# Where the expert weights' three loads stand at the end of the attention heads

## The chip, the core and the metric

The kernel runs on one core of a Trainium2 chip. TensorE (PE) multiplies and transposes, VectorE (DVE), ScalarE (ACT) and GpSimd (POOL) do the rest, and SyncE (SP) only issues DMAs. ACT and POOL issue DMAs too, between their own instructions and in order with them. The metric is the device time of one launch in microseconds, lower is better.

## The reference, cut to what matters

Two layers over x of shape (16, 256, 128), 4096 tokens. Each layer has an attention part and a feed-forward part, each added back to x under a gate. The first layer's attention has 16 heads of 8 dimensions with relative positions; its feed-forward part is a mixture of 8 experts, 2 of them chosen for each token:

```python
ctx = jnp.einsum('bhts,bshd->bthd', attn, v).reshape(b, t, d)
return ctx @ Wout.T + bout                       # first layer, attention
...
logits = xf @ router_w.T                         # router_w (8, 128)
g = jnp.einsum('nd,ehd->neh', xf, w_gate)        # w_gate (8, 256, 128) f32, 1 MiB
u = jnp.einsum('nd,ehd->neh', xf, w_up)          # w_up   (8, 256, 128) f32, 1 MiB
h = jax.nn.silu(g) * u
y = jnp.einsum('neh,edh->ned', h, w_down)        # w_down (8, 128, 256) f32, 1 MiB
```

The second layer has linear attention with four 128x128 weights and biases, and a feed-forward part with its own weights. They come much later in the kernel.

## The kernel before, in words

**Heads.** The 16 heads run one after the other on PE. Head h has 16 steps: `scores` (L1159, L1163), ACT's exponential (L858), and products with the values, `context_part` (L1181), after steps 11 and, for the head before, 3. Maxima for later heads (L1132, L1134, reduced by DVE in L1691, negated in L1700) are woven in; ACT sends the negated maxima into row 96 of the operand XC in two halves (`shift_row`, L816, tile name NEG), and the scores of steps 0 and 4 wait for them. The last maximum of the last head is the 8 H-th `max_mm`.

**Normalisation.** When the context of head h is complete, DVE copies it from PSUM to EV (`evacuate_context`, L1711). The copy waits until the numerators of head h - 2 have left the same buffer (`num_out`). Then for heads 0 to 14 POOL runs a chain, `sums_to_dram(h)` and `normalise(h)`:

1. the sums go to DRAM (L621) and come back spread over 128 partitions as RC (L623);
2. DVE takes the reciprocal (L1716). In DVE's program it stands at step 11 of head h + 1, behind that head's work, and for head 14 just ahead of `evacuate_context(15)`;
3. the reciprocals go to DRAM (L629) and come back broadcast over 32 partitions in four DMAs of 128 KB (L632);
4. POOL multiplies (L635, which counts `norm_done`) and sends the numerators to R1 in four DMAs (L638).

POOL begins the chain of head h + 1 only after that of head h.

**The tail.** Head 15 has the same chain with SP as the issuer: L496, L499, reciprocal L1784, L502, four broadcasts L506, DVE's multiplication L1787 (`t_norm`), and L510 for the numerators (`t_num_out`). After it ACT copies the context into OB (L877), PE applies the output projection (L1220), and the residual and the second layernorm follow.

**Expert weights.** After the last maximum SP issues at one go: the gate weights (L481), the up weights (L482), the down weights (L483), the router (L485), and eight small loads of the second layer (L487 to L491). All four expert loads count `ld_moe`, and PE waits for all of them once, ahead of its transposes (L1210, 12 chunks of four: 0 to 3 gate, 4 to 7 up, 8 to 11 down; then the router, L1213). For each chunk ACT makes the high part (L868, `m_ev`) and DVE the low part (L1778, `w_low`); two PSUM banks alternate, so PE's chunk c waits for the low part of chunk c - 2. DVE's order there is: `evacuate_context(15)`, low parts 0 to 3, reciprocal L1784, low parts 4 to 7, multiplication L1787, low parts 8 to 11, router. The operand buffers that WGN, WUN and WDN overlay are free from the last maximum on.

After L510 SP loads the second layer's feed-forward weights into FN (L517 to L520).

Of the kernel before, what the change touches and what calls it, by code (L numbers as in the profile page):

```python
# [22 lines left out]
H, DH = 16, 8  # L23
# [4 lines left out]
HID, E = 256, 8  # L28
# [57 lines left out]
def adaln_program(nc, a, out):  # L86
# [11 lines left out]
    def sb(name, shape, dt, ctx):  # L98
        return ctx.enter_context(nc.sbuf_tensor(name, shape, dt))

    def sem(name):
        return outer.enter_context(nc.semaphore(name))

    with outer:
# [12 lines left out]
        RN = sb("RN", [E, 128], F32, outer)  # L117
# [4 lines left out]
        WGN, WUN, WDN = (YY[:, N * i:N * i + N].bitcast(F32).rearrange("p (k d) -> p k d", k=16) for i in range(3))  # L122
# [68 lines left out]
        L1W = L1V[:, 0:512].rearrange("p (w d) -> p w d", w=4)  # L191
        BKV, BO1, BQ1 = L1V[:, 512:768], L1V[:, 768:896], L1V[:, 896:897]
# [49 lines left out]
        den_out, den_in, rec_ready, rec_out, rec_in, norm_done, num_out = (sem(s) for s in (  # L242
            "den_out", "den_in", "rec_ready", "rec_out", "rec_in", "norm_done", "num_out"))
        t_den_out, t_den_in, t_rec_out, t_rec_in, t_norm, t_num_out = (sem(s) for s in (
            "t_den_out", "t_den_in", "t_rec_out", "t_rec_in", "t_norm", "t_num_out"))
        o_in, o_mm, o_add = sem("o_in"), sem("o_mm"), sem("o_add")
        ld_moe, ld_l1, ld_ff = (sem(s) for s in ("ld_moe", "ld_l1", "ld_ff"))
        m_tr, m_ev, lg_mm, cmb = sem("m_tr"), sem("m_ev"), sem("lg_mm"), sem("cmb")
        gu_mm, sg_done, h_done, y_mm, acc_done = (sem(s) for s in ("gu_mm", "sg_done", "h_done", "y_mm", "acc_done"))
        l_q, l_ex, l_qd, l_kv, l_kvd, l_kk, l_kkd = (sem(s) for s in (  # L250
# [73 lines left out]
        def _(sp):  # L324
# [136 lines left out]
            for h in range(1, H):  # L461
# [12 lines left out]
                if h + 1 < H:  # L474
# [3 lines left out]
                    score_queries(h + 1)  # L478

            sp.wait_ge(max_mm, 8 * H)  # L480
            sp.dma_start(WGN[:, :, :], a["L0_ffn_w_gate"].rearrange("e (c p) d -> p (e c) d", p=128)).then_inc(ld_moe, 16)  # L481
            sp.dma_start(WUN[:, :, :], a["L0_ffn_w_up"].rearrange("e (c p) d -> p (e c) d", p=128)).then_inc(ld_moe, 16)  # L482
            sp.dma_start(WDN[:, :, :].rearrange("p (e c) k -> p e (c k)", e=E),  # L483
                         a["L0_ffn_w_down"].rearrange("e d k -> d e k")).then_inc(ld_moe, 16)
            sp.dma_start(RN[:, :], a["L0_ffn_router_w"]).then_inc(ld_moe, 16)  # L485
            for i, w in enumerate(("wq", "wk", "wv", "wo")):
                sp.dma_start(L1W[:, i, :], a["L1_attn_" + w]).then_inc(ld_l1, 16)  # L487
            sp.dma_start(BQ1, a["L1_attn_bq"].rearrange("(p o) -> p o", o=1)).then_inc(ld_l1, 16)
            sp.dma_start(BKV[:, 0:128], a["L1_attn_bk"].partition_broadcast(128)).then_inc(ld_l1, 16)
            sp.dma_start(BKV[:, 128:256], a["L1_attn_bv"].partition_broadcast(128)).then_inc(ld_l1, 16)  # L490
            sp.dma_start(BO1, a["L1_attn_bo"].partition_broadcast(128)).then_inc(ld_l1, 16)  # L491

            h, p = H - 1, (H - 1) % 2
            sp.wait_ge(ev_done, H)
# [14 lines left out]
            for g in range(4):  # L509
                sp.dma_start(R1[DH * h:DH * h + DH, :].rearrange("p (c g x) -> p c g x", c=4, g=4)[:, :, g],  # L510
                             EV[p][32 * g:32 * g + DH, :].rearrange("p (c x) -> p c x", c=4)).then_inc(t_num_out, 16)

            sp.wait_ge(zeroed, 9)
            for k, w in enumerate(("gate", "up")):
# [250 lines left out]
        def _(act):  # L765
# [96 lines left out]
                        shift_row(h + 1, (u - 3) // 3)  # L862

            for c in range(12):
                act.wait_ge(m_tr, c + 1)
                w, k4 = c // 4, slice(4 * (c % 4), 4 * (c % 4) + 4)
                t = banks[4 + c % 2][:, :].rearrange("p (w i) -> p w i", w=4)
                A(W2[w][:, 0, k4, :], t, ACT.Copy, scale=WS).then_inc(m_ev, 1)  # L868
# [172 lines left out]
        def _(pe):  # L1041
# [158 lines left out]
            context_part(H - 1, 1, 0)  # L1200
            context_part(H - 1, 1, 1)

            pe.wait_ge(ld_moe, 64)
            pe.wait_ge(max_done, 8 * H)
            for c in range(12):
                if c >= 2:
                    pe.wait_ge(w_low, c - 1)
                src = (WGN, WUN, WDN)[c // 4]
                for j in range(4):
                    last = tr(banks[4 + c % 2][:, 128 * j:128 * j + 128], src[:, 4 * (c % 4) + j, :], ident)  # L1210
                last.then_inc(m_tr, 1)
# [921 lines left out]
```

## Time and profile before

| what | before |
|---|---|
| median of 3 runs | 1026.28 us (1025.95 to 1028.13) |
| the profiled execution's own time | 1022.87 us |
| its span, first to last instruction | 1021.0 us |
| PE busy | 823.6 us (81%) |
| DVE busy | 722.0 us (71%) |
| ACT busy | 537.6 us (53%) |
| POOL busy | 410.8 us (40%) |
| mean granted TensorE clock | 0.912 of full speed |

Start times are microseconds from the start of the span. The heads end and the experts begin between about 420 and 505 us. The profiled execution is 3.41 us shorter than the median of the timed runs; differences within the profile are compared with each other, and carried over to the median.

### The profile page before, as it was taken

To read this page: it belongs to the slowest core of one execution; us is meant where nothing else is said; L and a number is where in the kernel's file an instruction comes from. 1 tells how busy PE (TensorE), PEld (TensorE's weight loads), DVE (VectorE), ACT (ScalarE), POOL (GpSimd) and SP (SyncE) were. 2 spreads that over 40 slices of the span, in tenths; PEclk is the share of its full clock that TensorE was granted. 3 is DMA by queue.
4 is the path that set the end of the run, shared out by engine and by line. 5 is a ranking of instruction groups with operands and counts; after the bars stand their busy time and mean duration, and the time that the engine had idled before them with its cause. 6 is when DMAs were issued, how large, how long until landed. Compare 5 with 4: busy or idle time off the path is not lost.

```text
span 1021.0 us, 23783 instructions
## 1 busy us (share of the span) xinstructions
PE 823.6 (81%) x9611; PEld 599.3 (59%) x9611; DVE 722.0 (71%) x1458; ACT 537.6 (53%) x985; POOL 410.8 (40%) x473
## 2 busy tenths in 40 slices
PE   2494699999999999975479998999998785257773
PEld 1253578888787878754246655666665474135563
DVE  6976366655555555325778898788787688899994
ACT  3860365767666766345445556566564644313332
POOL 5451724443344334344333235334443127214544
PEclk9696699999999999976599999999999798579998
DMA  8037523432343333631000000000000000000111
GB/s 137 11 76 240 131 54 77 100 84 68 78 100 82 72 73 82 164 84 32 1 1 2 2 1 1 2 1 2 1 2 2 0 1 1 0 1 11 21 22 32
DMA packets 55986, 47.17 MB, mean 46 GB/s; under 512 B 22284, under 2 KB 45012, under 8 KB 55156
## 3 DMA queue, kind: packets, MB, share of 16 engines
q1 hardware_dynamic: 36816, 26.24, 11.3%
q0 software_dynamic: 7424, 13.60, 5.6%
q10 hardware_dynamic: 11636, 5.80, 2.3%
q8 instruction: 76, 1.25, 0.5%
q14 instruction: 34, 0.28, 0.1%
HBM read 30.52 MB, written 12.06 MB: 42 GB/s over the span
## 4 chain that ended last, share of the span: by engine, by line
PE 52%; DVE 27%; DMA 5%; issue 5%; POOL 4%; ACT 4%; SPq 2%; POOLq 0%; DVEq 0%; ACTq 0%
PE PS L1159 12%; PE PS L1276 5%; PE PS L1278 5%; PE PS L1277 5%; PE PS L1163 5%; PE PS L1181 5%; PE PS L1132 5%; PE PS L1134 3%; DVE XX L1559 2%; DVE HB L1953 2%; PE PS L1076 2%; DVE XX L1565 2%; DVE AM L1550 2%; DVE ACC L1945 1%; DVE HQ L2082 1%
## 5 line engine op out<-in xcount | busy, mean ns | idle before, releaser
L1691 DVE TENSOR_REDUCE MX<-PS 128x4 f32<-128x1024 f32 x128 | 156.4, 1224 | 123.0 <-PE PS L1134 122.6
L858 ACT ACTIVATE REG<-PS 128x1024 f32<-128x1024 f32 x128 | 130.2, 1018 | 132.1 <-PE PS L1163 120.9
L1159 PE MATMUL PS<-XX,TB 96*128 96x64 f16 x2048 | 160.9, 247 | 5.8 <-issue 3.9
L683 POOL TENSOR_TENSOR HH<-HB,HH 128x512 f16<-128x512 f32 x64 | 75.5, 1180 | 172.4 <-ACT HH L909 172.4
L1159 PEld LDWEIGHTS PS<-XX,TB 96*128 96x128 f16 x2048 | 121.5, 120 | 34.8 <-issue 13.0
L939 ACT ACTIVATE SG<-PS 128x512 f32<-128x512 f32 x128 | 76.2, 595 | 110.6 <-PE PS L1278 110.3
L1953 DVE SCALAR_TENSOR_TENSOR HB<-PS,SG 128x512 f32<-128x512 f32 x128 | 87.8, 686 | 44.4 <-ACT SG L939 44.3
L1163 PE MATMUL PS<-XX,KC 97*128 97x128 f16 x1024 | 107.5, 228 | 0.0
L1276 PE MATMUL PS<-XH,XX 128*128 128x512 f16 x256 | 98.5, 385 | 10.1 <-DVE HB L1953 9.9
L1277 PE MATMUL PS<-XH,XX 128*128 128x512 f16 x256 | 97.9, 382 | 0.0
L1278 PE MATMUL PS<-XH,XX 128*128 128x512 f16 x256 | 97.8, 382 | 0.0
L1132 PE MATMUL PS<-TM,YY 64*64 64x256 f16 x1024 | 81.8, 335 | 18.3 <-DVE YY L1733 9.8
L831 ACT ACTIVATE YY<-YY,CON 128x256 f16<-128x256 f16 x224 | 96.2, 497 | 0.0
L1276 PE MATMUL PS<-XX,HH 128*128 128x128 f16 x512 | 89.7, 220 | 7.3 <-issue 2.7
L1278 PE MATMUL PS<-XX,HH 128*128 128x128 f16 x512 | 89.8, 220 | 0.0
L1277 PE MATMUL PS<-XX,HH 128*128 128x128 f16 x512 | 89.8, 220 | 0.0
L909 ACT ACTIVATE HH<-HB 128x512 f16<-128x512 f32 x128 | 79.8, 623 | 7.9 <-DVE HB L1953 7.6
L1440 PE MATMUL PS<-YY,XT 128*128 128x352 f32 x128 | 49.5, 536 | 35.7 <-DVE HQ L2082 35.7
L1163 PEld LDWEIGHTS PS<-XX,KC 97*128 97x128 f16 x1024 | 76.2, 113 | 0.0
L1132 PEld LDWEIGHTS PS<-TM,YY 64*64 64x64 f16 x1024 | 50.7, 187 | 34.1 <-issue 13.5
L1134 PE MATMUL PS<-KM,YY 64*64 64x256 f16 x1024 | 69.6, 287 | 0.0
L1945 DVE SCALAR_TENSOR_TENSOR ACC<-PS,CMBT,ACC 128x128 f32<-128x128 f32 x224 | 62.8, 344 | 1.1 <-PE PS L1278 0.9
(237 smaller groups left out, 1721.2 us busy)
## 6 DMA issues: line engine op xcount, KB each, us to landing
REG<-inverse_sums POOLq DMA_DIRECT2D x60, 128.0 KB, 2.9
KC<-keys_strips SPq DMA_DIRECT2D x16, 192.0 KB
keys_strips<-REG ACTq DMA_DIRECT2D x12, 224.0 KB
R<-in_L_attn_x SPq DMA_DIRECT2D x32, 64.0 KB, 3.6
XX<-NEG ACTq DMA_DIRECT2D x120, 1.0 KB, 2.2
R<-REG POOLq DMA_DIRECT2D x60, 32.0 KB, 2.8
queries_position<-REG ACTq DMA_DIRECT2D x2, 896.0 KB
XX<-queries_position SPq DMA_DIRECT2D x56, 32.0 KB
```

Of the source, the lines that this page charges most:

```text
L831: last = A(to, queries, ACT.Copy, scale=CON[:, C_OWN + 8 - 8 * (piece // 8) + j:C_OWN + 9 - 8 * (piece // 8) + j])
L858: A(P[jt][:, 1024 * up:1024 * up + 1024].rearrange("p (k x) -> p k x", k=2), ST[u % 2], ACT.Exp).then_inc(exp_done, 1)
L909: A(HH[k % 4][:, 0, :], HB[k % 2][:, :], ACT.Copy).then_inc(hi_done, 1)
L1132: mm(o, yp[rows, a], TM[p][rows, 31 - a:31 - a + T], start=True, stop=False)
L1134: last = mm(o, yc[rows, a], KM[p][rows, :], start=False, stop=True)
L1159: mm(o_pos[:, a], TB[p][0:96, y0:y0 + 128], xp[0:96, 8 * bank + a], start=(a == 0), stop=False, skip_group_check=True)
L1163: last = mm(o[:, 128 * c:128 * c + 128].rearrange("p (b s a) -> p b s a", b=4, s=4), KC[p][0:97, c, 128 * jt:128 * jt + 128], xc[0:97, c, ...
L1276: mm(o, w[0], x[0], start=first, stop=False)
L1277: mm(o, w[0], x[1], start=False, stop=False)
L1278: return mm(o, w[1], x[0], start=False, stop=final)
L1691: nc.vector.tensor_reduce(MX[h % 2][:, :].rearrange("p (r a) -> p r a", r=2)[:, :, 2 * g:2 * g + 2], PS[:, bank:bank + 2, :].rearrange("p ...
L1953: STT(HB[k % 2][:, :], banks[2 + k % 2], 1.0 / WS, SG[k % 2][:, :], ALU.mult, ALU.mult).then_inc(hb_done, 1)
```

## The change

`ld_moe` becomes three semaphores. SP still issues the gate weights after the last maximum, and the router right behind them. It then waits for `norm_done` of 14, that is until POOL has multiplied head 13, and issues the up weights. The down weights are issued by ACT, between its high parts of chunks 3 and 4, after a wait for `norm_done` of 15 (head 14 multiplied). The eight small loads of the second layer move behind the tail's last DMA (L510), ahead of the FN loads. PE waits for gate and router before chunk 0, for up before chunk 4, and for down before chunk 8.

```diff
@@ sync
             sp.wait_ge(max_mm, 8 * H)
-            sp.dma_start(WGN[:, :, :], a["L0_ffn_w_gate"].rearrange("e (c p) d -> p (e c) d", p=128)).then_inc(ld_moe, 16)
-            sp.dma_start(WUN[:, :, :], a["L0_ffn_w_up"].rearrange("e (c p) d -> p (e c) d", p=128)).then_inc(ld_moe, 16)
-            sp.dma_start(WDN[:, :, :].rearrange("p (e c) k -> p e (c k)", e=E),
-                         a["L0_ffn_w_down"].rearrange("e d k -> d e k")).then_inc(ld_moe, 16)
-            sp.dma_start(RN[:, :], a["L0_ffn_router_w"]).then_inc(ld_moe, 16)
-            for i, w in enumerate(("wq", "wk", "wv", "wo")):
-                sp.dma_start(L1W[:, i, :], a["L1_attn_" + w]).then_inc(ld_l1, 16)
-            sp.dma_start(BQ1, a["L1_attn_bq"].rearrange("(p o) -> p o", o=1)).then_inc(ld_l1, 16)
-            sp.dma_start(BKV[:, 0:128], a["L1_attn_bk"].partition_broadcast(128)).then_inc(ld_l1, 16)
-            sp.dma_start(BKV[:, 128:256], a["L1_attn_bv"].partition_broadcast(128)).then_inc(ld_l1, 16)
-            sp.dma_start(BO1, a["L1_attn_bo"].partition_broadcast(128)).then_inc(ld_l1, 16)
+            sp.dma_start(WGN[:, :, :], a["L0_ffn_w_gate"].rearrange("e (c p) d -> p (e c) d", p=128)).then_inc(ld_gate, 16)
+            sp.dma_start(RN[:, :], a["L0_ffn_router_w"]).then_inc(ld_gate, 16)
+            sp.wait_ge(norm_done, H - 2)
+            sp.dma_start(WUN[:, :, :], a["L0_ffn_w_up"].rearrange("e (c p) d -> p (e c) d", p=128)).then_inc(ld_up, 16)
...
                 sp.dma_start(R1[DH * h:DH * h + DH, :].rearrange("p (c g x) -> p c g x", c=4, g=4)[:, :, g],
                              EV[p][32 * g:32 * g + DH, :].rearrange("p (c x) -> p c x", c=4)).then_inc(t_num_out, 16)
+            for i, w in enumerate(("wq", "wk", "wv", "wo")):
+                sp.dma_start(L1W[:, i, :], a["L1_attn_" + w]).then_inc(ld_l1, 16)
+            sp.dma_start(BQ1, a["L1_attn_bq"].rearrange("(p o) -> p o", o=1)).then_inc(ld_l1, 16)
+            sp.dma_start(BKV[:, 0:128], a["L1_attn_bk"].partition_broadcast(128)).then_inc(ld_l1, 16)
+            sp.dma_start(BKV[:, 128:256], a["L1_attn_bv"].partition_broadcast(128)).then_inc(ld_l1, 16)
+            sp.dma_start(BO1, a["L1_attn_bo"].partition_broadcast(128)).then_inc(ld_l1, 16)
@@ scalar
             for c in range(12):
+                if c == 4:
+                    act.wait_ge(norm_done, H - 1)
+                    act.dma_start(WDN[:, :, :].rearrange("p (e c) k -> p e (c k)", e=E),
+                                  a["L0_ffn_w_down"].rearrange("e d k -> d e k")).then_inc(ld_down, 16)
                 act.wait_ge(m_tr, c + 1)
@@ tensor
-            pe.wait_ge(ld_moe, 64)
             pe.wait_ge(max_done, 8 * H)
             for c in range(12):
                 if c >= 2:
                     pe.wait_ge(w_low, c - 1)
+                if c == 0:
+                    pe.wait_ge(ld_gate, 32)
+                elif c % 4 == 0:
+                    pe.wait_ge((ld_up, ld_down)[c // 4 - 1], 16)
```

## Rows read from the trace of the kernel before

**Rows 1.** The chain that ended last, 400 to 520 us: start, us, what
```profile
422.45 5.36 DMA inverse_sums<-RC
...
429.56 8.95 DMA REG<-inverse_sums
...
449.22 1.90 DMA sums<-REG
451.14 3.55 DMA RC<-sums
454.71 0.36 DVE RC L1784
455.09 1.41 DMA inverse_sums<-RC
...
467.91 1.07 ACT REG L877
```

**Rows 2.** Timeline of POOL, 427 to 461 us: start, length, idle before and releaser
```profile
428.09 1.96 POOL L632 DMA_DIRECT2D REG<-inverse_sums  x4 [5.08 <-DMA inverse_sums<-RC]
438.58 2.36 POOL L635 TENSOR_TENSOR REG<-REG 128x1024 f32<-128x1024 f32 x1 [8.53 <-DMA REG<-inverse_sums]
441.23 2.25 POOL L638 DMA_DIRECT2D R<-REG  x4 [0.29 <-POOL REG L635]
443.47 0.58 POOL L621 DMA_DIRECT2D sums<-REG  x1
445.86 0.60 POOL L623 DMA_DIRECT2D RC<-sums  x1 [1.81 <-DMA sums<-REG]
448.41 0.56 POOL L629 DMA_DIRECT2D inverse_sums<-RC  x1 [1.95 <-DVE RC L1716]
450.40 1.96 POOL L632 DMA_DIRECT2D REG<-inverse_sums  x4 [1.42 <-DMA inverse_sums<-RC]
455.21 2.35 POOL L635 TENSOR_TENSOR REG<-REG 128x1024 f32<-128x1024 f32 x1 [2.85 <-DMA REG<-inverse_sums]
```

**Rows 3.** DMA queues, 422 to 425, then 425 to 428 us: packets, MB, share
```profile
q1 hardware_dynamic: 368, 0.75, 95.9%
...
q1 hardware_dynamic: 441, 0.87, 103.3%
q0 software_dynamic: 32, 0.02, 2.4%
```

**Rows 4.** DMA queues, 428 to 433, then 433 to 436 us
```profile
q1 hardware_dynamic: 1134, 1.38, 104.8%
q10 hardware_dynamic: 320, 0.00, 4.2%
...
q0 software_dynamic: 181, 0.51, 70.8%
q1 hardware_dynamic: 365, 0.23, 35.3%
```

**Rows 5.** Timeline of PE about the end of the heads
```profile
432.45 0.34 PE L1159 MATMUL PS<-XX,TB 96*128 96x64 f16 x3 [0.98 <-DMA XX<-NEG]
...
443.77 1.93 PE L1181 MATMUL PS<-REG,V 128*32 128x256 f32 x32 [1.11 <-ACT REG L858]
...
455.67 1.97 PE L1210 MATMUL PS<-CON,YY 128*128 128x128 f32 x8 [1.33 <-DVE XX L1778]
```

**Rows 6.** Timeline of DVE, 447 to 464 us, and where FN is first read
```profile
447.76 0.35 DVE L1716 RECIPROCAL RC<-RC 128x32 f32<-128x32 f32 x1 [14.99 <-DMA RC<-sums]
...
458.30 0.69 DVE L1778 SCALAR_TENSOR_TENSOR XX<-PS,XX 128x512 f16<-128x512 f32 x1 [0.16 <-ACT XX L868]
461.46 1.23 DVE L1787 TENSOR_TENSOR REG<-REG 128x1024 f32<-128x1024 f32 x1 [2.47 <-DMA REG<-inverse_sums]
...
561.42 0.95 DVE L1550 TENSOR_REDUCE YY<-YY 128x48 f32<-128x768 f32 x1
```

**Rows 7.** Timeline of SP's queue, 420 to 467 us
```profile
420.52 0.84 SPq L481 DMA_DIRECT2D YY<-in_L_ffn_w_gate  x1
...
424.12 3.43 SPq L483 DMA_DIRECT2D YY<-in_L_ffn_w_down  x1
...
429.38 0.43 SPq L487 DMA_DIRECT2D YY<-in_L_attn_wk  x1
...
456.52 1.71 SPq L506 DMA_DIRECT2D REG<-inverse_sums  x4
```

**Rows 8.** ACT: its timeline at chunk 4; lines L845, L952 (ns min/median/max, starts)
```profile
453.52 0.60 ACT L868 ACTIVATE XX<-PS 128x512 f16<-128x512 f32 x1 [1.08 <-PE PS L1210]
...
L845 ACTq DMA_DIRECT2D queries_position<-REG x2: 808/860/912, 91.5 to 92.5; - x2
...
L952 ACT ACTIVATE EX<-PS,YY x8: 677/687/688, 790.0 to 817.2; 128x512 f32<-128x512 f32 x8
```

More of the change, by code:

```diff
@@ L246, in adaln_program @@
         o_in, o_mm, o_add = sem("o_in"), sem("o_mm"), sem("o_add")
-        ld_moe, ld_l1, ld_ff = (sem(s) for s in ("ld_moe", "ld_l1", "ld_ff"))
+        ld_gate, ld_up, ld_down, ld_l1, ld_ff = (sem(s) for s in ("ld_gate", "ld_up", "ld_down", "ld_l1", "ld_ff"))
         m_tr, m_ev, lg_mm, cmb = sem("m_tr"), sem("m_ev"), sem("lg_mm"), sem("cmb")
```

## Prediction

> **What bounds the kernel now.** I read the page first: PE is busiest, but the slices around 420 to 500 us are where it idles, and the change touches only them. Then I read the chain that ended last [rows 1]. It leaves PE at 422 us and follows DMAs: head 13's reciprocals to DRAM (5.36 us) and their broadcast back (8.95 us), then POOL's chain for head 14, then the tail, until ACT starts on the output projection at 467.91. From there everything is a chain of engines on this start. So the change is worth what it moves 467.91.
>
> POOL's timeline puts a price on the DMAs [rows 2]. Head 14's chain runs beside almost nothing: from the issue of L629 to that of L632 1.99 us (448.41 to 450.40), from there to the multiplication 4.81 us. Head 13's same steps took 5.64 (422.45 to 428.09, [rows 1, 2]) and 10.49 us. The excess is 3.65 + 5.68 = 9.33 us. The DMA queues say why: the four 128 KB broadcasts, issued from 428.09, moved nothing on q0 until 433, and then 0.51 MB in 3 us [rows 4]. Until then q1 moved the weights: 0.75 MB by 425, 1.62 MB by 428, 3.00 MB by 433 [rows 3, 4], and three loads of 1 MiB are 3.15 MB. The broadcasts started when what had been issued before them was through.
>
> After that, head 14's reciprocal on DVE (447.76) is what the copy of head 15 stands behind [rows 6]. PE had finished that head at 443.77 + 1.93 = 445.70 [rows 5]. The copy's successor L496 starts at 449.22 [rows 1].
>
> **Gate alone.** At 0.89 MB in 3 us [rows 3] a load of 1.05 MB takes 3.5 us; with 0.75 MB moved by 425 the gate weights are through at 426.0, 5.5 us after their issue at 420.52 [rows 7]. L629 of head 13 is issued at 422.45, inside it. It can't land faster than about 1.4 us, as L502's [rows 1] nor slower than the 5.36 it took with three loads. Its 32 packets fell between 425 and 428 [rows 3], so most of the wait was the gate load and stays: I take 4.3, landing 426.75. Issue of the broadcasts 0.28 later (as 427.81 to 428.09), 4.81 to the multiplication: 431.84 instead of 438.58, and `norm_done` 14 with its end 2.36 later, 434.20 instead of 440.94.
>
> PE gains too. It stood 0.98 us before the scores at 432.45 for the negated maxima [rows 5], which ACT sent during the loads: 320 packets of q10 came only after 428 [rows 4]. With the load through at 426 they are there before 431.47. PE ends the heads 1.0 us earlier, about 444.7, as ACT's exponentials, the only other thing it waits for there, move with it.
>
> **Up behind `norm_done` 14.** SP issues it at 434.25. While SP stands in this wait nothing else is queued there but the tail, which can't start before 446; so the wait costs nothing. The load runs until about 434.25 + 5.5 = 439.75, and PE needs it for chunk 4 after 449. But it meets POOL's L638 of head 13 (434.5 to 436.75) and L621 of head 14 (436.75), which took 2.1 us alone (443.47 to 445.86 less 0.28, [rows 2]). By the same reading as above L621 takes 2.1 to 5.4; I take 4.3 again: 441.05. Then [rows 2] L623 at 441.3; L629 2.55 later, 443.9; broadcasts 445.9; multiplication 450.7; `norm_done` 15 at 453.0 instead of 457.56. The reciprocal of head 14 comes 1.90 after L623 (445.86 to 447.76), at 443.2, done 443.6: before PE is. So DVE's copy of head 15 starts at PE's end, 444.75, takes 1.17, and L496 starts at 446.0 instead of 449.22. **The tail starts 3.2 us earlier.** This term is firm: POOL's chain may slip by a further 1 us before it is touched.
>
> **The tail and the down load.** From L496 to L506 it was 7.30 us (449.22 to 456.52), including 3.55 for L499 beside the broadcasts of head 14, which it meets again (445.9 to 449, one step earlier). L506 comes at 453.3. ACT reaches its new wait at about 449.5 (chunk 3's high part, moved forward by 3.2), stands there for `norm_done` 15 at 453.0, and issues. So 1 MiB and the four broadcasts are issued within 0.3 us of one another. The delay of the broadcasts is the unknown of this case. Nothing, if they are served beside the load or before it; 3.5 us, the whole load, if they stand behind it, as head 13's did [rows 4]. The last of four is issued 1.3 us after the first, when the load is certainly in, and all of them must land. So I go by [rows 4], not by zero, and take 2.2, since the first ones and the load's last packets can overlap. Multiplication L1787 at 453.3 + 4.94 + 2.2 = 460.4, 1.0 us before 461.46 [rows 6].
>
> The Trainium skill (DMA: Bandwidth & Descriptors, section Queues, rings and completion order) says that each DMA engine goes round-robin between the queue rows that have work, packet by packet. By that the broadcasts on SP's row lose next to nothing to a load on ACT's row, the delay is near zero and the tail keeps what it gained. The packets of [rows 4] do not look like it: q0 had work from 428.09 and got no turn before 433.
>
> **ACT and the weights.** The issue itself keeps ACT: 0.86 us as for ACT's two DMAs of L845, 896 KB each by the page's last part [rows 8], at most 3.43 as for SP's third load [rows 7]. Until it is done chunks 4 to 7 stand. Both of PE's chunks 4 and 5 are ready by then. After them, PE's chunk 6 started at 455.67 and DVE's low part of chunk 7 ended at 458.99 [rows 5, 6], 3.3 us; ACT's 0.60 and DVE's 0.69 for chunk 4 ahead of it [rows 6, 8] make 4.6 and with the hops between them 4.7 us from ACT's start to the low part of 7: 453.9 + 4.7 = 458.6. (In the trace it is 5.5, 453.52 to 458.99, with the reciprocal between, which is earlier now.) L1787 stands behind it on DVE. It is hidden under 460.4, and caps any gain at 461.46 - 458.6 = 2.8 us. At 3.43 the cap is 0.3 us. Down lands at about 459, and its chunks 8 to 11 run beside L1787 and L510 as they did.
>
> **The second layer's small loads.** Seven of 64 KB and one of 0.5 KB, 0.46 MB, go behind L510. Eight issues of about 0.45 us (L487 took 0.43, [rows 7]) put the FN loads 3.6 us later. The numerators' DMAs are issued before them, as they were before the FN loads, so the collision is the same. Their users come long after: FN is first read at 561.42 [rows 6], the second layer's biases at 790 [rows 8]. Nothing. The router's 4 KB ride behind the gate weights instead of behind all three, also nothing: its chunk is PE's last.
>
> **Sum.** -3.2 + 2.2 = -1.0 us, on 1022.87 of the profiled execution 1021.9, on the median 1025.3. The smallest change that a measurement of this kernel tells from none is about 0.2%, 2.05 us.
>
> **Rivals.**
> - *The down load costs the tail nothing* (served packet by packet beside it, or issued after the broadcasts). Gain 3.2, capped by DVE's order at 2.8: 1023.5. For it: the two are issued on different queues and at nearly one time, and a later `norm_done` 15 puts the load behind. Against: [rows 4]. But a later one also brings the cap down. 0.30.
> - *The whole gain is given back.* Down goes in first and delays the broadcasts by the 3.5 us, or L502 ahead of them: multiplication at 461.7, +0.3, 1026.5. 0.20.
> - *Slower: ACT's wait.* If the up load does to head 14's chain what the three did to head 13's, and `norm_done` 15 comes at 457.6 as before, ACT goes on at 458.5 and L1787 can't start before 463.2: 1.8 us later, 1028.1; with an issue of 3.43 us 4.3 later, 1030.6. It decides from `norm_done` 15 at 455.8 on, 2.8 us later than I have it. Against: head 14's broadcasts are issued at 445.9, 6 us after the up load is through. 0.10.
> - The forecast, part of the load's time lost, keeps 0.40.
>
> **Range and chances.** The unknown delay (0 to 3.5, cap 2.8) spans 1023.5 to 1026.6. With the landings between 1.4 and 5.4 that put down before or behind the tail, and the slower rival's near end, 1022.9 to 1027.6; the forecast's own case alone, a delay of 1.2 to 3.2, is 1024.3 to 1026.3. Faster by over 0.2% needs a gain of 2.05: the first rival and the edge of the forecast, 0.33. Slower: 0.10 and the edge of the second, 0.13. The same: 0.54.
>
> **What the profile would show.** Head 13's L635 at 431 to 433 instead of 438.58. The scores at 431.5 without a wait on NEG. L496 near 446.0, released by PE through L1711. L506 near 453.3, and L1787 between 458.6 and 461.7; what released it, the broadcasts or the low part of chunk 7, tells the forecast from the cap. ACT idle from 449.5 to 453. I am wrong if L1787 starts before 458.6, if `norm_done` 15 is far from 453, or if the 5.2 us from L1787's end (462.69) to ACT's start (467.91) [rows 1, 6] change.

## The result

The changed kernel takes 1028.72 us (median of 8 runs, 1026.58 to 1031.74) where the kernel before takes 1026.12 in the same comparison. The ratio is 1.0031, interval 1.0017 to 1.0045: slower by 3.2 us by the ratio, 2.6 by the medians. I had forecast 1025.3, 1.0 us faster, in a range up to 1027.6. The direction and the range were wrong.

The chain that ended last, of the changed kernel (start, us, what), answers to [rows 1]:

```profile
421.95 4.95 DMA inverse_sums<-RC
...
428.65 3.29 DMA REG<-inverse_sums
432.01 2.36 POOL REG L636
434.65 2.25 POOL R L639 x4
436.90 6.73 DMA sums<-REG
443.90 1.88 DMA RC<-sums
...
453.73 2.35 POOL REG L636
456.10 8.96 DMA YY<-in_L_ffn_w_down
465.20 1.10 PE PS L1218 x4
...
470.56 1.07 ACT REG L882
```

Head 13's broadcasts land in 3.3 us after the last issue instead of 8.95, as hoped. But the chain no longer runs through the tail at all. It goes from POOL's multiplication of head 14 to the down load, waits 8.96 us for it to land, and then through PE's chunks 8 to 11. ACT begins the output projection at 470.56, with nothing awaited but its own last conversion.

ACT, DVE, PE and SP of the changed kernel there (timelines; L873 is the high part, L1786 the low part, L1218 the transposes, L1795 the multiplication of the tail):

```profile
444.78 1.08 ACT L873 ACTIVATE XX<-PS 128x512 f16<-128x512 f32 x2 [2.61 <-PE PS L1218]
...
449.46 0.60 ACT L873 ACTIVATE XX<-PS 128x512 f16<-128x512 f32 x1 [0.28 <-PE PS L1218]
456.10 0.49 ACTq L868 DMA_DIRECT2D YY<-in_L_ffn_w_down  x1
456.63 1.09 ACT L873 ACTIVATE XX<-PS 128x512 f16<-128x512 f32 x2 [6.58 <-POOL REG L636]
...
470.48 0.18 ACT L875 ACTIVATE RT<-PS 128x8 f16<-128x8 f32 x1 [0.35 <-PE PS L1221]
470.56 2.04 ACT L882 ACTIVATE REG<-R 128x512 f32<-128x512 f32 x2
```

```profile
445.81 0.35 DVE L1724 RECIPROCAL RC<-RC 128x32 f32<-128x32 f32 x1 [13.55 <-DMA RC<-sums]
446.08 1.16 DVE L1719 COPY REG<-PS 128x1024 f32<-128x1024 f32 x1
...
460.65 0.69 DVE L1786 SCALAR_TENSOR_TENSOR XX<-PS,XX 128x512 f16<-128x512 f32 x1 [0.16 <-ACT XX L873]
461.25 1.22 DVE L1795 TENSOR_TENSOR REG<-REG 128x1024 f32<-128x1024 f32 x1
466.95 0.69 DVE L1786 SCALAR_TENSOR_TENSOR XX<-PS,XX 128x512 f16<-128x512 f32 x1 [4.48 <-ACT XX L873]
```

```profile
442.22 1.93 PE L1186 MATMUL PS<-REG,V 128*32 128x256 f32 x32 [1.11 <-ACT REG L859]
...
465.20 1.94 PE L1218 MATMUL PS<-CON,YY 128*128 128x128 f32 x8 [5.22 <-DMA YY<-in_L_ffn_w_down]
```

```profile
434.44 0.75 SPq L484 DMA_DIRECT2D YY<-in_L_ffn_w_up  x1
447.27 0.59 SPq L489 DMA_DIRECT2D sums<-REG  x1
```

Read against [rows 5, 6]: ACT stands 6.58 us for `norm_done` 15. DVE's L1795 has no DMA as its releaser any more; it starts when the low part of chunk 7 is done. PE then stands 5.22 us for the down load.

The profiles differ by up to 5 us ahead of the change, so from here on I count from the issue of the gate load. These marks are worked out from each run's timelines (us after that issue):

| kernel | head 14's sums issued | landed | tail starts | tail's multiplication | router converted | ACT starts projection | ratio to before (interval) |
|---|---|---|---|---|---|---|---|
| before | 22.95 | 25.3 | 28.70 | 40.94 | 45.66 | 47.39 | |
| changed | 16.88 | 23.9 | 27.25 | 41.23 | 50.46 | 50.54 | 1.0031 (1.0017 to 1.0045) |
| x7_down_unread | 17.06 | 24.3 | 27.72 | 43.12 | 47.83 | 49.23 | 0.9990 (0.9966 to 1.0014) |
| x8_no_down_load | 16.86 | 23.7 | 27.12 | 40.59 | 45.30 | 46.62 | 0.9975 (0.9958 to 0.9992) |
| x1_down_no_wait | 17.31 | 23.7 | 27.25 | 44.39 | 49.11 | 50.47 | 1.0011 (0.9994 to 1.0028) |
| z1_down_alone_moved | 20.33 | 22.8 | 26.97 | 44.01 | 50.03 | 50.44 | 1.0025 (1.0008 to 1.0042) |
| x3_small_back | 18.91 | 25.2 | 28.78 | 42.79 | 52.43 | 52.50 | 1.0052 (1.0035 to 1.0070) |
| x4_small_alone | 21.62 | 24.0 | 27.48 | 39.78 | 44.50 | 45.88 | 0.9980 (0.9965 to 0.9996) |
| x5_up_after_sums | 16.93 | 19.7 | 25.45 | 39.22 | 47.71 | 47.78 | 1.0002 (0.9982 to 1.0022) |
| x2_down_behind_up | 17.31 | 24.9 | 28.45 | 40.34 | 45.06 | 46.44 | 1.0005 (0.9984 to 1.0025) |
| v1_both_after_broadcasts | 17.40 | 25.5 | 28.86 | 41.60 | 46.31 | 47.70 | 0.9986 (0.9969 to 1.0002) |
| v5_both_behind_issue | 17.34 | 21.6 | 25.45 | 37.81 | 42.53 | 43.93 | 0.9962 (0.9942 to 0.9981) |
| y1_down_by_act | 17.33 | 19.8 | 25.46 | 41.12 | 45.83 | 47.21 | 1.0011 (0.9993 to 1.0028) |

("Landed" is where POOL issues the next step.) Each ratio compares a kernel with the kernel before in the same round of timed runs. The medians of before in these rounds are 1026.12, 1025.90, 1025.38 and 1024.89 us, so the ratios can be compared from run to run, and the plain times cannot. Each mark comes from a single execution. From before to changed the last mark moves by +3.15 us, as the time does; in other runs mark and ratio differ by up to 2.9 us (x7). The ratios say how much a version gains or loses, the marks say where. An interval that holds 1 means that the version is not told from before.

### The profile page after: what moved, and what is told of

Its sections match the earlier page's. It is cut to its first block, busy times and chain, and to the rows that moved or that the text cites. A ratio compares the mean times of both kernels' runs of the same rounds, so it can differ in the third digit from the quotient of the medians.

```text
span 1024.7 us, 23785 instructions
## 1 busy us (share of the span) xinstructions
PE 823.6 (80%) x9611; PEld 599.0 (58%) x9611; DVE 722.3 (70%) x1458; ACT 537.5 (52%) x985; POOL 411.5 (40%) x473
## 4 chain that ended last, share of the span: by engine, by line
PE 53%; DVE 26%; DMA 5%; issue 5%; POOL 4%; ACT 4%; SPq 2%; POOLq 0%; DVEq 0%; ACTq 0%
PE PS L1164 12%; PE PS L1284 6%; PE PS L1286 5%; PE PS L1285 5%; PE PS L1168 5%; PE PS L1137 5%; PE PS L1186 5%; PE PS L1139 3%; DVE XX L1567 2%; DVE HB L1961 2%; PE PS L1081 2%; DVE XX L1573 2%; DVE AM L1558 2%; DVE ACC L1953 1%; DVE HQ L2090 1%
```

## The experiments

The first four ask whether the down load's landing, ACT's wait, or something behind 470 us is the loss.

**x7_down_unread.**

```diff
-                elif c % 4 == 0:
-                    pe.wait_ge((ld_up, ld_down)[c // 4 - 1], 16)
-                src = (WGN, WUN, WDN)[c // 4]
+                elif c == 4:
+                    pe.wait_ge(ld_up, 16)
+                src = (WGN, WUN, WGN)[c // 4]
...
                 last.then_inc(o_mm, 1)
+            pe.wait_ge(ld_down, 16)
```

> The changed kernel, but PE transposes the gate weights once more for chunks 8 to 11, so nothing in the weights' chain waits for the down load; the load itself stays where it is and is waited for after the output projection. What is left out: the down weights never enter the products. Theory A (the load's landing holds PE's chunk 8, 5.22 us in the changed kernel, and through it ACT's start on the output projection): ACT starts L882 when the numerators land, near 467.6 instead of 470.56, and the time falls by about 3 us, to 1025.7. Theory B (ACT's wait for norm_done 15 delays chunks 4 to 7 and so DVE's multiplication): that wait is still here, L1795 stays at 461.3 and the time within 0.5 us of the changed kernel's 1028.7. Theory C (the loss lies behind 470 us: small loads, clock): also unchanged, 1028.7.

1024.86 us, ratio 0.9990. The loss is gone, as theory A has it: by the ratio nothing of it lies behind 470 us. But its profile shows a part that I had not expected:

```profile
464.73 1.23 DVE L1796 TENSOR_TENSOR REG<-REG 128x1024 f32<-128x1024 f32 x1 [1.26 <-DMA REG<-inverse_sums]
```

ACT starts at 49.23, not at 47.5: in this execution it took 7.5 us from the issue of the tail's broadcasts to the multiplication at 43.12, beside the load, where it had been 4.94 before (456.52 to 461.46, [rows 6, 7]). So the load has two ways to hold the end, its own landing and the broadcasts' delay.

**x1_down_no_wait.**

```diff
                 if c == 4:
-                    act.wait_ge(norm_done, H - 1)
                     act.dma_start(WDN[:, :, :].rearrange("p (e c) k -> p e (c k)", e=E),
```

> The changed kernel without ACT's wait for norm_done 15: the down load goes out at about 450.1, after the high part of chunk 3. Theory A: it lands by 459, before PE's chunk 8 asks for it, and the held chunks go too; it now runs beside head 14's broadcasts and the tail's first DMAs, which costs the tail 1 to 3 us. Time 1025 to 1027.5, so faster than the changed kernel. Theory C: 1028.7 as before.

1027.47 us, ratio 1.0011: the slow end of what I expected. The load is issued at 449.62. PE still stands 2.75 us for it ahead of chunk 8, but this is off the chain that ends last, which runs through the tail. The load stands ahead of the tail's later DMAs. SP's timeline of this run:

```profile
453.52 0.33 SPq L495 DMA_DIRECT2D inverse_sums<-RC  x1
458.35 1.72 SPq L499 DMA_DIRECT2D REG<-inverse_sums  x4
465.64 3.02 SPq L503 DMA_DIRECT2D R<-REG  x4
```

The write of 16 KB (L495) took 4.81 us, where it had taken 1.41 in [rows 1], and the step from L499 to the multiplication took 6.03 us instead of 4.94. This is the second way by itself: the load delays the tail's small DMAs. It delayed head 14's broadcasts too. It was issued 1.2 us after the first of POOL's four, and these took 8.40 us from their first issue to the multiplication, where head 14's took 5.29 in the changed kernel.

**x3_small_back.** The eight small loads again right behind the router, otherwise as changed (the diff is cut):

```diff
             sp.dma_start(RN[:, :], a["L0_ffn_router_w"]).then_inc(ld_gate, 16)
+            for i, w in enumerate(("wq", "wk", "wv", "wo")):
+                sp.dma_start(L1W[:, i, :], a["L1_attn_" + w]).then_inc(ld_l1, 16)
...
             sp.wait_ge(norm_done, H - 2)
```

> The changed kernel with the eight small loads back behind the router load. Theory A: they share the DMA engines with head 13's broadcasts (issued 427.2), which land 1 to 1.5 us later; POOL's chain, norm_done 15 and with it the down load follow, 1029.7. Theory C (their new place behind L503 hurts the numerators or what comes later): faster than the changed kernel by 1 us or more.

1030.49 us, ratio 1.0052: 2.1 us slower than the changed kernel. The direction is that of theory A, the size twice my estimate. Head 13's multiplication comes at 14.04 instead of 11.99, and the marks behind it 1.4 to 2.0 us later, the down load's issue too (37.63 against 36.08, then 9.34 us to its landing). Moving the small loads behind the tail was the good part of the change.

**x4_small_alone.** The kernel before, with only this part of the change: the eight small loads behind the tail's last DMA.

```diff
             sp.dma_start(RN[:, :], a["L0_ffn_router_w"]).then_inc(ld_moe, 16)
-            for i, w in enumerate(("wq", "wk", "wv", "wo")):
-                sp.dma_start(L1W[:, i, :], a["L1_attn_" + w]).then_inc(ld_l1, 16)
...
                              EV[p][32 * g:32 * g + DH, :].rearrange("p (c x) -> p c x", c=4)).then_inc(t_num_out, 16)
+            for i, w in enumerate(("wq", "wk", "wv", "wo")):
+                sp.dma_start(L1W[:, i, :], a["L1_attn_" + w]).then_inc(ld_l1, 16)
...
```

> The kernel before with only the eight small loads moved behind L510. My reading of the queues: 0.46 MB less beside head 13's broadcasts, which land 1.5 to 2 us earlier; head 14's reciprocal moves by the same, from 447.76 to about 446, where PE's end of head 15 (445.7) becomes the bound: 1 to 2 us faster, 1024.5. Theory C: no gain or a loss, 1026.1 or more.

1023.92 us, ratio 0.9980: 2 us faster, inside the forecast. I had costed this part at nothing in the prediction, and looked only at where the loads went, not at what they left: head 13's broadcasts. The gain was not missing from the sum, though. The gate term took 4.81 us for these broadcasts, as if nothing ran beside them, and so held it without a name.

The next four ask what the up load costs, and where both loads could stand.

**x5_up_after_sums.**

```diff
-            sp.wait_ge(norm_done, H - 2)
+            sp.wait_ge(den_out, 16 * (H - 1))
             sp.dma_start(WUN[:, :, :], a["L0_ffn_w_up"].rearrange("e (c p) d -> p (e c) d", p=128)).then_inc(ld_up, 16)
```

> The changed kernel, but SP issues the up load when head 14's sums are in DRAM (L622 landed) instead of behind norm_done 14. Theory A has two parts: the up load costs L622 of head 14 some 4.5 us (6.73 against 2.1), and the down load's landing sets the end. By the first part L622 goes back to about 2.1 us and the next step L624 takes the load's collision, with a head start of under 0.5 us, so head 14's reciprocal comes 1 to 2 us earlier than 445.8; by the second part ACT's start on the output projection follows norm_done 15 and the down load, so 1 to 2 us earlier too: 1027.2. If the up load had nothing to do with L622's 6.73 us, nothing moves: 1028.7.

1026.12 us, ratio 1.0002, about 3 us faster than the changed kernel. Head 14's sums take 2.7 us to POOL's next step instead of 7.0, and the next step 3.3 instead of 1.9. The tail starts at 25.45, bounded by PE (DVE's copy of head 15 stands for PE's last products at 444.04). This is the 3.2 us that I had promised for the change itself. And ACT still starts at 47.78, behind the router's conversion at 47.71: the down load's landing takes it back.

**x2_down_behind_up.**

```diff
             sp.dma_start(WUN[:, :, :], a["L0_ffn_w_up"].rearrange("e (c p) d -> p (e c) d", p=128)).then_inc(ld_up, 16)
+            sp.dma_start(WDN[:, :, :].rearrange("p (e c) k -> p e (c k)", e=E),
+                         a["L0_ffn_w_down"].rearrange("e d k -> d e k")).then_inc(ld_down, 16)
```

and ACT's wait and DMA taken out.

> The changed kernel with the down load issued by SP right behind the up load, both behind norm_done 14, and none by ACT. Theory A: no load stands in the tail any more, PE's chunk 8 doesn't wait; but L622 of head 14 stands behind or among 2 MiB, 8 to 10 us instead of 6.7, so the tail starts 2 to 3 us later than in the changed kernel and then runs undisturbed. ACT's start on the output projection about 1 us earlier than the changed kernel's: 1027.5. If ACT's wait and the held chunks were all the loss, the time falls to that of before or under, 1025 to 1026.

Ratio 1.0005 (0.9984 to 1.0025), 1024.86 us. By the ratio it lies between the two expectations. The steps are not those of theory A: the tail starts 1.2 us later than in the changed kernel, not 2 to 3, and ACT 4.1 us earlier, not 1. 2 MiB delay head 14's sums by only 0.6 us more than 1 MiB did (7.6 against 7.0). The queues suggest why: 652 packets of SP's queue moved between 442 and 444 us, after POOL's queue, which the sums share, had moved its last before 442, so part of the second load stood behind the sums.

**v1_both_after_broadcasts.** As x2, with the wait `sp.wait_ge(rec_in, 64 * (H - 2))` in place of `norm_done`, so both loads are issued when head 13's broadcasts have landed.

> Up and down loads from SP when head 13's broadcasts have landed (rec_in of 14 heads), some 3 us ahead of norm_done 14. Theory A: 2 MiB run from 433 to 440, L622 of head 14 (issued near 437) lands by 442 to 443 and its reciprocal comes at 444.5 to 445.5, close to PE's end; the tail is undisturbed. ACT's start near 465 to 466: 1 to 2 us faster than before, 1024.5. If a load beside POOL's chain costs nothing as long as it is not issued ahead of it, the gain is the full 3 us, 1023.

1024.23 us, ratio 0.9986 (0.9969 to 1.0002): not told from before, and near my first expectation. ACT starts at 47.70, no better than before's 47.39: head 14's sums took 8.1 us, issued behind the two loads, where I had expected them to land 2 to 3 us earlier.

**v5_both_behind_issue.** As x2, but SP waits for a semaphore that POOL counts right after issuing head 13's four broadcasts.

```diff
                                  rec_d[p, 1024 * g:1024 * g + 1024].partition_broadcast(32)).then_inc(rec_in, 16)
+                if h == H - 3:
+                    gp.sem_inc(sent, 1)
                 gp.wait_ge(rec_in, 64 * (h + 1))
@@ sync
-            sp.wait_ge(norm_done, H - 2)
+            sp.wait_ge(sent, 1)
```

> Up and down loads from SP as soon as POOL has issued head 13's four broadcasts (a semaphore that POOL counts after them), about 429.2. Theory A (what is issued first is served first): the broadcasts land as in the changed kernel, within 0.5 us; 2 MiB are through by 437.5, so L622 of head 14 takes 2 to 4 us, its reciprocal is done before PE's end at 444, the tail starts at about 445.4 and nothing stands in it. ACT's start on the output projection near 464.2: 3 us faster than before, 1023. Against it (packets of all queues share the engines): the broadcasts slow down by 2 to 3 us, POOL's chain moves back, 1025.

1021.84 us, ratio 0.9962: 3.9 us faster than before, 7 us faster than the change. It is the version to keep. POOL, SP and ACT of this run:

```profile
424.12 1.97 POOL L635 DMA_DIRECT2D REG<-inverse_sums  x4 [4.41 <-DMA inverse_sums<-RC]
429.68 2.35 POOL L640 TENSOR_TENSOR REG<-REG 128x1024 f32<-128x1024 f32 x1 [3.59 <-DMA REG<-inverse_sums]
432.32 2.26 POOL L643 DMA_DIRECT2D R<-REG  x4 [0.29 <-POOL REG L640]
434.57 0.58 POOL L624 DMA_DIRECT2D sums<-REG  x1
438.83 0.60 POOL L626 DMA_DIRECT2D RC<-sums  x1 [3.68 <-DMA sums<-REG]
```

```profile
425.46 0.75 SPq L484 DMA_DIRECT2D YY<-in_L_ffn_w_up  x1
426.26 2.68 SPq L485 DMA_DIRECT2D YY<-in_L_ffn_w_down  x1
442.68 0.60 SPq L491 DMA_DIRECT2D sums<-REG  x1
```

```profile
461.16 2.04 ACT L882 ACTIVATE REG<-R 128x512 f32<-128x512 f32 x2 [1.22 <-DMA R<-REG]
```

SP issues the two loads at 425.46 and 426.26, while POOL's four issues run from 424.12 to 426.09. They cost the broadcasts little: from the first issue to the multiplication it is 5.56 us, against 4.84 in the changed kernel, and 5.53 in x2, where no load ran there. The multiplication comes at 12.45 against 11.99. The burst issued ahead of them in the kernel before cost them 5.7.

The last three take the down load's place apart.

**y1_down_by_act.** v5 with the down load put back to ACT, at chunk 4 behind `norm_done` 15.

> The last version (up and down behind the issue of head 13's broadcasts) with only the down load put back where the change has it: ACT, at chunk 4, behind norm_done 15. The tail keeps its early start. Theory A (landing of the down load sets the end): norm_done 15 is 33.8 us after the gate load's issue, the load lands 9 us later, PE's chunk 8 waits for it and the weights' chain ends at 48.3, where it was 42.5; ACT's start on the output projection is 4.4 us later than in that version, 1 us later than before: 1026.4. If the down load's place costs nothing, 1021.8.

1025.28 us, ratio 1.0011. The price of that place is 5.0 us by the ratios of this and v5, 0.9962 (0.9942 to 0.9981) against 1.0011 (0.9993 to 1.0028), and 3.3 us by ACT's start. The expected 4.4 lies between, but the way is the other one. With POOL's chain undisturbed, `norm_done` 15 comes at 31.5, and the load is issued 0.7 us ahead of the first of the tail's broadcasts (31.53 and 32.23):

```profile
YY<-in_L_ffn_w_down ACTq DMA_DIRECT2D x1, 1024.0 KB, 7.0
REG<-inverse_sums SPq DMA_DIRECT2D x4, 128.0 KB, 7.2
```

(DMA issues, 450 to 465 us; the last number is the median from issue to landing.) The broadcasts take 7.2 us; DVE's multiplication comes at 41.12 instead of v5's 37.81:

```profile
463.32 1.22 DVE L1797 TENSOR_TENSOR REG<-REG 128x1024 f32<-128x1024 f32 x1 [4.38 <-DMA REG<-inverse_sums]
```

The queues show the order, as [rows 4] did. From 455 to 458 us the load's queue (q10) moved 781 packets and SP's queue, with broadcasts issued from 454.43 on, none.

**x8_no_down_load.** The changed kernel with ACT's wait kept, without the load, chunks 8 to 11 from the gate weights.

```diff
                     act.wait_ge(norm_done, H - 1)
-                    act.dma_start(WDN[:, :, :].rearrange("p (e c) k -> p e (c k)", e=E),
-                                  a["L0_ffn_w_down"].rearrange("e d k -> d e k")).then_inc(ld_down, 16)
```

> The changed kernel with ACT's wait for norm_done 15 kept, but no down load at all; PE transposes the gate weights once more for chunks 8 to 11. What is left out: loading and using the down weights. It parts the wait from the traffic. Theory A: with the load gone, the held chunks 4 to 7 alone put DVE's multiplication at 41.2 us after the gate load's issue (0.3 later than before), and ACT's start on the output projection at 46.5, 0.9 earlier than before or equal: 1025 to 1026. Theory B (ACT's wait is the loss): 1028.7 as the changed kernel.

1022.78 us, ratio 0.9975. The wait by itself is not the loss. ACT stands 5.63 us there, DVE's multiplication L1793 starts directly behind the low part of chunk 7 (458.84), and the projection at 46.62, 0.8 earlier than before. Theory B is out. The wait is not free either: the multiplication comes 5.74 us after the issue of the tail's broadcasts, where DMAs alone bounded it at 4.94 before, so DVE's order cost about 0.8 us of gain.

**z1_down_alone_moved.** The kernel before, with only the down load moved to ACT behind `norm_done` 15; PE's first wait counts three loads, chunk 8 waits for `ld_down`.

> The kernel before with only the down load moved to ACT, at chunk 4 behind norm_done 15; gate, up, router and the small loads stay in one burst. Theory A: the burst is 3.5 us shorter, so head 13's broadcasts and POOL's chain are 3.5 us earlier and the tail starts about 2 us earlier; but the down load lands 9 us after norm_done 15 (33.5 + 9 = 42.5 after the gate load's issue) and ACT's start on the output projection is near 48.2 against 47.4: 1027. So the placement alone turns a gain of 2 us into a loss of 1. If it does not hold anything, 1024.

1028.31 us, ratio 1.0025 (1.0008 to 1.0042). The tail starts 1.7 us earlier, and both ways of loss act together:

```profile
464.59 1.23 DVE L1791 TENSOR_TENSOR REG<-REG 128x1024 f32<-128x1024 f32 x1 [3.71 <-DMA REG<-inverse_sums]
```

```profile
465.32 1.94 PE L1214 MATMUL PS<-CON,YY 128*128 128x128 f32 x8 [5.80 <-DMA YY<-in_L_ffn_w_down]
```

I had expected a smaller loss (48.2 for ACT's start; it is 50.44). The load went out at 35.07 instead of 33.5 and took 9.5 us instead of 9, so the weights' chain by itself ends at 50.03. The broadcasts' delay, which I had not counted, brings the numerators' landing to the same place: from the issue of the tail's broadcasts to the multiplication it is 9.76 us against 4.94, with the load issued 0.8 us after the first of the four. ACT waits for the numerators last, by 0.2 us.

## Why the prediction was wrong

**Gate alone: right.** Landing of L629's successor 4.95 us (I took 4.3), multiplication of head 13 at 11.99 after the gate load's issue (I had 431.84, which is 11.32), and no wait of PE for the negated maxima. PE ends its heads 1.05 us earlier (442.22 + 1.93, against 445.70, less 0.5 by which this execution is ahead).

**"L621 takes 2.1 to 5.4; I take 4.3": mis-sized.** It took 6.73, beyond my upper end. The upper end was 5.36, one wait in the trace of before, of a write that was issued 1.9 us behind the gate load. I treated it as a bound, and it was one sample. So head 14's reciprocal came at 445.81, 1.7 us after PE's end (444.15), and the term that I had called firm, the tail 3.2 us earlier, was 28.70 - 27.25 = 1.45. x5 shows the cause: with the up load issued after L622 landed, the step falls to 2.7 and the tail starts 3.25 us earlier.

**"Down lands at about 459, and its chunks 8 to 11 run beside L1787": the step that decides.** I took 5.5 us from issue to the end of a 1 MiB load, from 0.75 MB moved by 425 and the rate after. Where a semaphore of its own now shows it, a landing takes 8.8 us for the up load and 9.0 for the down load (in the other runs 6.1 to 9.3 for the up load, and 7.0 to 9.5 for the down load where ACT issues it). The queues of the changed kernel, 457 to 462 and then 462 to 465 us:

```profile
q10 hardware_dynamic: 965, 0.99, 78.0%
q1 hardware_dynamic: 110, 0.28, 18.8%
q0 software_dynamic: 31, 0.04, 3.0%
...
q0 software_dynamic: 97, 0.09, 18.6%
q1 hardware_dynamic: 59, 0.05, 12.3%
q10 hardware_dynamic: 75, 0.06, 11.9%
```

94% of the bytes had moved by 462, 5.9 us after the issue. The load landed at 465.06, after a last 0.06 MB beside POOL's numerators. In the kernel before four loads share one semaphore and PE comes to it long after, so its trace shows no landing of a single load, and I put the mean rate in its place. From chunk 8 to the router's conversion it is 5.28 us (465.20 to 470.48), so chunk 8 had until about 462.4 before it would hold ACT, 3.4 us of cover over my 459. A landing time 3.5 us longer and a `norm_done` 15 3.6 us later (36.06 after the gate load's issue instead of 453.0 - 420.52 = 32.48) used it up: a cost of nothing became PE's 5.22 us, and 470.56 instead of the numerators' landing, which was due about 5.2 us after L1795's end, near 467.7. This is 2.9 us; the other 0.3 of the 3.15 is the multiplication's. My sign of being wrong, that the 5.2 us from the multiplication's end to ACT's start change, came: they are 8.09 (462.47 to 470.56).

**The delay of the tail's broadcasts: the mechanism was right, the 2.2 us not met.** In the profiled changed kernel it did not show, since DVE's order was the later: the load went out 1.06 us after their first issue, and the multiplication came 6.21 us after it, behind the low part of chunk 7. In y1, where the load is 0.7 us ahead, it is 3.9 us in the step from L499 to the multiplication (8.89 us against 4.94), and in z1 4.8 us: I had 3.5 as the upper end. The rule of the Trainium skill (DMA: Bandwidth & Descriptors, section Queues, rings and completion order), turns packet by packet, by which I reckoned a delay near zero (not the 2.2 that I took), is not borne out by y1 and z1. In y1 the broadcasts' queue moved no packet for 3 us; in z1, from 458 to 461 us, it moved 33 against the load's 756. Why is not shown.

**DVE's cap: right.** ACT goes on at 456.63, the low part of chunk 7 ends at 461.34: 4.71 us, I had 4.7. By this the multiplication was 0.3 us later than before. The rival that ended slower rested on it. Its condition came true (`norm_done` 15 at 456.08, from 455.8 on), but this part was worth 0.3 us. That its 1028.1 us lies near the measured time is luck: the loss was the landing, and x8, with the wait and without the load, is faster than before.

**The small loads: "nothing" was wrong.** x4 and x3 show a gain of 2 us from taking them away behind head 13's broadcasts, which the gate term held without naming it. In all, the gain that was there to have is v5's 3.9 us, and the change ended 3.2 us on the other side. From the changed kernel to y1 only the up load moves, and from y1 to v5 only the down load. By the ratios the up load's place is 2.1 us of these 7.1 and the down load's 5.0; by ACT's start they are 3.3 and 3.3. Taken in another order the shares differ: from the changed kernel to x2 only the down load moves, for 2.7 us by the ratios, since it then stands behind head 14's sums.

**What stays open.** How the loss divides between landing and broadcasts from execution to execution: the profiles of the changed kernel and of x7 show one each, and x7's profile (49.23) is worse than its ratio suggests. Whether the queue matters beside the order of issue: the cheap loads of v5 are SP's beside POOL's broadcasts, the dear ones of x1, x7, z1 and y1 are ACT's, and no run puts a load on ACT right behind the last broadcast. From ACT's start to the end of the span the stretch is 553.1 us before, 554.1 changed and 552.9 to 556.8 in the others, without a link to the edits that I could show.

## What to carry to other kernels

- Give every load that matters a semaphore of its own before costing a move. Bytes over rate say when most of a load is through, not when it lands; here that was 5.9 us against 9.0.
- In these runs a bulk load was cheap when it was issued with or after the last of a group of broadcasts and nothing followed for as long as it ran (v5), and dear when it was issued before them (y1) or after the first and before the last of the four (x1, x7, z1: 2.6 to 4.8 us). Hook it to the issue of the last small DMA, not to its landing or to the work behind it.
- When loads are moved, price what they leave as well as where they go, as a term of its own.

## What the hardware showed that I had not expected

- 2 MiB issued with the last of four 128 KB broadcasts cost these at most 0.7 us (v5); 1 MiB issued 0.7 us ahead of them, on another engine's queue, cost 3.9 us (y1), and issued 0.8 to 1.2 us after the first of them 4.8 (z1), 2.6 (x7) and 3.1 (x1). In the changed kernel, x3 and x5, with the load 1.1 to 1.4 us after the first, it was at most 1.3 to 1.5 us, hidden behind DVE's order.
- A small write of 16 KB behind a 1 MiB load took 4.8 us (x1) to 6.7 us (changed), and behind 2 MiB 7.3 (x2) to 7.8 (v1). The second load added 0.6 to 1.1 us. In v5, where the 2 MiB were issued 8 to 9 us ahead, the write took 4.0.
